# Turning a group's negated maxima with one matmul and eight transfers in a Trainium2 attention and feed-forward kernel

## The reference

```python
att = jnp.einsum('bhqd,bhkd->bhqk', q, k) * scale
causal = jnp.tril(jnp.ones((t, t), dtype=bool))
att = jnp.where(causal, att, -jnp.inf)
att = jax.nn.softmax(att, axis=-1)
y = jnp.einsum('bhqk,bhkd->bhqd', att, v)
```

## Time and profile before

| what | value |
|---|---|
| time, median of 3 runs | 2168.74 us (2168.48 to 2174.09) |
| span of the profiled execution | 2166.8 us |
| PE busy | 2118.4 us, 98% of the span |
| PEld busy | 1878.8 us |
| ACT busy | 1316.1 us, 61% |
| DVE busy | 1259.9 us, 58% |
| POOL busy | 492.9 us, 23% |
| DMA queue of SP (q1) | 91912 packets, 152.75 MB |

### The profile page before, as it was taken

How to read it: one execution, slowest core, us unless ns; L and a number is a source line. 1 busy time by engine, 2 the same in 40 slices (tenths; PEclk the granted TensorE clock), 3 DMA queues, 4 the chain that set the end, 5 groups by cost and what they waited for, 6 DMA issues and landing times.

```text
span 2166.8 us, 52048 instructions
## 1 busy us (share of the span) xinstructions
PE 2118.4 (98%) x16294; PEld 1878.8 (87%) x16294; DVE 1259.9 (58%) x3928; ACT 1316.1 (61%) x2807; POOL 492.9 (23%) x899
## 2 busy tenths in 40 slices
PE   8789999999999999999999999999999999999998
PEld 4368889989889888899989889988999898988998
DVE  7765555556555565556556565565556556565452
ACT  6456566666556666566666666666566666656553
POOL 2222122221222222122221122222122132122220
PEclk9889999999999999999999999999999999999999
DMA  8742332232322332332232322333232232321100
GB/s 275 239 120 63 77 71 70 61 81 64 90 65 61 82 74 69 75 69 73 61 81 64 90 64 62 81 76 73 71 76 70 56 82 69 83 64 37 37 6 10
DMA packets 95940, 167.69 MB, mean 77 GB/s; under 512 B 19204, under 2 KB 38404, under 8 KB 95672
## 3 DMA queue, kind: packets, MB, share of 16 engines
q1 hardware_dynamic: 91912, 152.75, 28.6%
q10 hardware_dynamic: 3760, 11.54, 1.5%
HBM read 98.26 MB, written 68.17 MB: 77 GB/s over the span
## 4 chain that ended last, share of the span: by engine, by line
PE 89%; DVE 1%; DMA 0%; issue 0%; SPq 0%; ACT 0%; POOL 0%; POOLq 0%; DVEq 0%
PE ring L1241 44%; PE ring L1226 10%; PE pM L1116 7%; PE pS L1104 6%; PE pO L1164 6%; PE ring L1254 5%; PE ring L1176 4%; PE ring L1206 2%; PE ring L1196 2%; PE ring L1148 1%; PE ring L1215 1%; DMA qk_d<-c 0%; SPq L614 0%; DVE full_g L960 0%; DMA Qs<-nm 0%
## 5 line engine op out<-in xcount | busy, mean ns | idle before, releaser
L921 DVE CUSTOM_DVE_ANT_0 pM<-pM,mask 128x512 f32<-128x512 f32 (+3 forms) x1024 | 498.7, 502 | 366.1 <-PE pM L1116 292.3
L1241 PE MATMUL ring<-Yhi,H 128*128 128x256 f32 x1984 | 501.7, 289 | 0.0
L1241 PE MATMUL ring<-Xhi,H 128*128 128x256 f32 x1984 | 497.9, 288 | 0.0
L1241 PE MATMUL ring<-Ylo,H 128*128 128x256 f32 x1984 | 489.2, 282 | 0.0
L1241 PE MATMUL ring<-Xlo,H 128*128 128x256 f32 x1984 | 486.4, 282 | 0.0
L1241 PEld LDWEIGHTS ring<-Ylo,H 128*128 128x128 f32 x1984 | 377.8, 190 | 7.2 <-issue 3.4
L1241 PEld LDWEIGHTS ring<-Yhi,H 128*128 128x128 f32 x1984 | 377.0, 190 | 7.1 <-issue 3.4
L1241 PEld LDWEIGHTS ring<-Xlo,H 128*128 128x128 f32 x1984 | 379.1, 191 | 0.8
L1241 PEld LDWEIGHTS ring<-Xhi,H 128*128 128x128 f32 x1984 | 378.4, 191 | 1.0 <-issue 0.2
L1116 PE MATMUL pM<-Ks,Qs 128*128 128x512 f32 x992 | 304.2, 340 | 20.6 <-DVE mx L921 9.0
L865 ACT ACTIVATE Yhi<-ring,cols 128x256 fp32r<-128x256 f32 x248 | 117.8, 475 | 266.8 <-PE ring L1241 170.1
(11 more groups left out here) (146 smaller groups left out, 3518.7 us busy)
## 6 DMA issues: line engine op xcount, KB each, us to landing
qk_d<-c SPq DMA_DIRECT2D x120, 256.0 KB, 3.4
Qs<-qk_d SPq DMA_DIRECT2D x120, 192.0 KB
Ks<-qk_d SPq DMA_DIRECT2D x120, 192.0 KB
qk_d<-c SPq DMA_DIRECT2D x120, 128.0 KB, 3.0
xTs<-in_xT SPq DMA_DIRECT2D x16, 512.0 KB, 4.3
raw<-in_h SPq DMA_DIRECT2D x8, 1024.0 KB, 10.4
xz<-in_x SPq DMA_DIRECT2D x16, 512.0 KB, 3.9
H<-raw ACTq DMA_DIRECT2D x8, 1024.0 KB, 9.3
```

Of the source, the lines that this page charges most:

```text
L921: nc.vector.tensor_tensor_reduce(pM[:, h % 2, 0:n], pM[:, h % 2, 0:n], mask[:, T - n:T], 1.0, NEG, ALU.add, ALU.max, mx[:, t, h:h + 1]).th ...
L1241: mm = nc.tensor.matmul(to, w, x_part, start=(k == 0 and m == 0), stop=(k == KB - 1 and m == 1))
```

## The change

`mhl` is laid out head first, `[128, G, 2, TB]`, so that its 32 columns can be the weights of one matmul. The result has 32 rows (head j, part n, block t) of 128 queries in place of 8 rows of 512. ACT copies 32 x 128. Since a row of the stack now lies in four rows of `nm`, each head's two rows are moved by two transfers, each from four partitions of 128 numbers to one partition of 512: eight transfers for a group, 128 on `nm_in`. The head of the program keeps its way; its copies add 128 where they added 64.

```diff
-NM_ROWS = 2 * G
+NM_ROWS = 2 * G * TB
...
-        nm = sb("nm", [NM_ROWS, T], F32R)
-        m_wide = over(nc, nm_at, "m_wide", [P, TB, P], F32R)
+        m_wide = sb("m_wide", [P, TB, P], F32R)
+        nm = over(nc, nm_at, "nm", [NM_ROWS, P], F32R)
...
-        mx, mhl = sb("mx", [P, TB, G]), sb("mhl", [P, TB, 2 * G], F32R)
+        mx, mhl = sb("mx", [P, TB, G]), sb("mhl", [P, G, 2, TB], F32R)
...
+        NM_COPIES = 16 * 2 * G
...
                         for j in range(G):
-                            at = SROWS * (j % 2)
-                            sp.dma_start(Q[at:at + 2, j // 2, j % 2].bitcast(F32),
-                                         nm[j:NM_ROWS:G].bitcast(F32)).then_inc(nm_in, 16)
+                            for n in range(2):
+                                at, rows = SROWS * (j % 2) + n, slice((2 * j + n) * TB, (2 * j + n + 1) * TB)
+                                sp.dma_start(Q[at:at + 1, j // 2, j % 2].bitcast(F32).rearrange("n (t q) -> n t q", t=TB),
+                                             nm[rows].bitcast(F32)).then_inc(nm_in, 16)
...
-                            for p, (landed, n) in enumerate(((nm_in, 64), (nm_done, 1))):
+                            for p, (landed, n) in enumerate(((nm_in, NM_COPIES), (nm_done, 1))):
...
-                        need(act, nm_in, (b * NG + g) * 64)
-                        nc.scalar.activation(nm[:], ring[0:NM_ROWS, BANKS[kind, off, a]], ACT.Copy).then_inc(nm_done, 1)
+                        need(act, nm_in, (b * NG + g) * NM_COPIES)
+                        nc.scalar.activation(nm[:], ring[0:NM_ROWS, BANKS[kind, off, a], 0:P], ACT.Copy).then_inc(nm_done, 1)
...
-                        top, rest = (m_wide[:, :, n::32] if steps is HEAD else mhl[:, :, n * G:(n + 1) * G] for n in range(2))
+                        top, rest = (m_wide[:, :, n::32] if steps is HEAD else mhl[:, :, n].rearrange("p j t -> p t j") for n in range(2))
...
-                            pe.wait_ge(nm_in, (b * NG + g + 1) * 64)
+                            pe.wait_ge(nm_in, (b * NG + g + 1) * NM_COPIES)
...
-                        for t in range(TB):
-                            mm = nc.tensor.matmul(to[0:NM_ROWS, t * P:(t + 1) * P], mhl[:, t], ident[:],
-                                                  start=True, stop=True)
-                        mm.then_inc(nt_ready, 1)
+                        nc.tensor.matmul(to[0:NM_ROWS, 0:P], mhl[:].rearrange("p j n t -> p (j n t)"), ident[:],
+                                         start=True, stop=True).then_inc(nt_ready, 1)
```

## The result

The changed kernel takes 2294.41 us (median of 5 runs, 2291.23 to 2297.26) against 2168.74 us for the kernel before (median of 5, 2167.25 to 2174.09). The ratio is 1.058, with a 95% interval of 1.0565 to 1.059: 5.8% slower.

What follows compares the result with a forecast made beforehand. PE's instruction stream was taken as the bound. 57 stalls of 1.87 us (106.6 us) less 10.4 us saved gave 96.2 us more on the 2166.8 us span; with 1.9 us added, 2265 us, 4.4% slower, range 2197 to 2306.

Steps and rivals of the forecast that it cites:

- an issue of 0.70 us: Dear issue on SP: 657 ns and 0.04 between, eight take 5.6 us, 41 us more, 2306 us; inside the 0.82 case.
- stretches of 0.50 behind the stalls: Sign against the prediction: granted PE clock at 0.50 behind stalls; it expected 1.00 throughout.
- PE saves 0.18 us a group: On PE, four matmul starts become one, saving three of 0.06 us; over 58 groups 10.4 us.
- Eight issues at 0.61 us: On SP, each transfer's issue with its gap takes 0.61 us, so the last of eight ends 2.44 us later.
- the nearest rows (563 and 557): Basis for the new transfer's issue cost on SP: present two-row transfer 563 ns, four rows of `den_d` 557 ns.
- the rival of the cheap issue: SP's eight issues at 303 ns and 0.04 between take 2.75 us; kernel gains, 2159 us; chance 0.06.
- The margins: Slack before each group's first `exp` on PE: 0.90, 0.30, 0.13, 0.44 us in groups 2, 3, 0, 1; mean stall 1.87 us.
- The copy at 0.29 us: On ACT, the copy shrinks from 512 to 128 columns and takes about 0.29 us, a saving of 0.29.
- the falling clock: Rival: after each of 57 stalls PE loses half of 3.4 us at low clock; 97 us more, 2362 us; chance 0.06.
- all 57 stalls alike: In the sum, every group but the roomy one stalls PE by the mean of 1.87 us, 106.6 us.
- Nothing behind the transfers on SP: SP work queued behind the transfers, the saves of `qk` in group 3, waits 1.2 us late and costs nothing.
- PE gives nothing back: With PE busy 130.0 of 130 us in the steady part, no idle time absorbs the stalls; nothing counted.

Runs made afterwards that it cites:

- four: The changed kernel with its one matmul and 32 x 128 copy, but one transfer per head, four a group: 2159.87 us, timed again 2162.58 us.
- filler: The changed kernel with eight needless 256-column matmuls on PE ahead of the wait for the maxima: 2269.86 us, ratio 1.0468.
- per_head: The changed kernel, all eight issues on SP, but one semaphore per head; each of the first four `exp` units waits for its own head only: 2186.92 us.
- rows8: The kernel before with only its transfers doubled, eight of one row each, four matmuls and 8 x 512 copy kept: 2336.1 us, ratio 1.077.
- per_head_g1: The changed kernel with a semaphore for each head, and in group 1 only four transfers in place of eight: 2165.90 us, ratio 0.9988.
- two_queues: The changed kernel with its eight transfers split, four issued by SP and four by ACT right behind its copy: 2235.27 us, ratio 1.0311.

## Why the prediction was right, and what it missed

The prediction said 2265 us with a range of 2197 to 2306; 2294.41 lies in it, 29 us above the forecast. Its mechanism, the wait for the last of eight serial issues, is what the runs show. That the number stayed inside the range is in part luck: the upper end was set by an issue of 0.70 us, which didn't come, and the room it left was taken up by the clock, which the range had left out. By one of its own signs, stretches of 0.50 behind the stalls, the prediction was wrong. Point by point:

- **PE saves 0.18 us a group.** Right: 0.06 us for the one matmul, and `four` shows 6 to 9 us by itself where the sum had 10.4.
- **Eight issues at 0.61 us.** Right for groups 2, 3 and 0: 4.96 to 5.01 us for eight, where the sum had 4.88, and a median of 573 ns. In group 1 the eight took 5.41 us. The choice of the nearest rows (563 and 557) over the ends at 342 and 657 held; the rival of the cheap issue fell. The Trainium skill's account of where a small transfer's time goes ("DMA: Bandwidth & Descriptors", Anatomy of one DMA — SWDGE (gpsimd) path), most of it in the write receipt and little in making the descriptors, is for the other way of issuing. Taken over to SP's queue it would have made the change a gain, and there the measurement decides against it: each issue held SP for 573 ns and the next began after it.
- **The margins.** Right. The four stalls less the four savings were to lengthen a pass by 4 x 1.87 - 4 x 0.18 = 6.76 us. The pass without a low clock is 6.72 us longer, and those of `filler`, also at the full clock, 6.6 us in the mean. PE's idle times of 1.17, 1.71 and 1.68 us in groups 2, 3 and 0, and of 1.87 or 2.38 us in group 1 (predicted 1.43, 1.85, 2.02 and 2.18), leave out the modelled tail of the matmul ahead.
- **The copy at 0.29 us.** It is 0.26.
- **The clock.** This is the step that was mis-sized. I gave the falling clock 0.06 as a case of its own, all 57 stalls or none, 97 us, and counted nothing of it in the sum. It came in part: 14 stretches. `filler`, with 13 fewer, takes 24.5 us less, of the 29 us by which the forecast was short; 13 times half of 3.4 us is 22 us of it.
- **The end of the program.** The sum treated all 57 stalls alike. Behind the last start of group 2's matmul, where two stalls remain, they are 2.76 and 2.30 us, and PE is idle for 18.2 us against 11.4 before: 6.8 us more, where the sum had 3.7. That is 3 us of the rest.
- **Nothing behind the transfers on SP.** That step looked at group 3 alone and was wrong for group 1. The effect was real, 21 us in `per_head`, but in the changed kernel ACT waited for the denominators' move for only 2.9 us, against 21.9 us in `per_head`, since PE's own stall came first; so the sum did not suffer. That was luck, as the step had not been worked out.
- **PE gives nothing back.** Right: in the pass at the full clock PE is busy for 129.93 of 136.36 us, where it was busy for all of 129.64, so the stalls stand in the time in full.

That most of the extra time is the wait for the last of eight serial issues is shown from three sides: the same number of transfers without the rest of the change (`rows8`), the rest with half the transfers (`four`), and the same transfers with a narrower wait (`per_head`, `per_head_g1`).

## What to carry to other kernels

Ask of each transfer on a path not how many bytes it has but how many issues stand in the queue until the last one that somebody waits for; here each cost 0.61 us, and trading three matmuls of 0.06 us for four of them lost wherever PE waited for the last one. Where the consumer needs the first piece first, give the pieces their own semaphores, and look at what stands behind the added issues before counting them as free. And price a stall on TensorE together with what the clock does after it: here about a fifth of the loss was work at 1.2 GHz.

## What was not expected of the hardware

- A transfer that gathers eight partitions of 512 bytes into two rows takes 612 ns to issue in the median (`four`), against 563 ns for two whole rows: four times the pieces for 49 ns.
- The single-row transfers of `rows8` took 589 ns each in the median, more than the 573 ns of the ones that gather four partitions, and up to 1627 ns. The two lines, `four` first:

```profile
L615 SPq DMA_DIRECT2D Qs<-nm x232: 597/612/1142, 167.4 to 2006.3; - x116
L615 SPq DMA_DIRECT2D Qs<-nm x464: 518/589/1627, 169.3 to 2183.2; - x155
```

- SP's issues are slower while ACT issues too: 696 ns in the median in `two_queues`, and 588 ns for the 28 that have little or nothing of ACT's issues beside them. ACT's own show no such difference: 613 ns beside SP's, 631 ns for the 23 others. The Trainium skill ("Trainium Kernel Development and Optimization", Key Constraints) says that issuing from several engines saves only the issue time on the sequencer; the trace does not contradict it, and shows that SP gives some of that time back.
